# One-core Mamba block with a mixture of experts: five tables of slots respread (norms, outputs, experts' projections, scaled inputs)

## What is computed

```python
h = _layernorm(x) * (1 + ca) + sa
xn = layernorm(h) * norm_g + norm_b
# for each direction (forward, and backward on the flipped rows), 256 inner columns, 16 states:
u, z = split(xn @ Win.T);  u = silu(conv4(u) + convb)
dtr, Bm, Cm = split(u @ Wx.T);  dt = softplus(dtr @ Wdt.T + bdt)
h_t = exp(dt_t * A) * h_(t-1) + dt_t * u_t * B_t        # 512 steps
y_t = sum_n h_t * C_t;  y = (y + u * D) * silu(z) @ Wout.T
x = x + ga * (h + y_fwd + y_bwd)
h = _layernorm(x) * (1 + cb) + sb
w = top-2 softmax gates of h @ gate_w over 8 experts, 0 elsewhere
x = x + gb * (sum_e w_e * swiglu(h, ew1, ew2, ew3)[e] + swiglu(h, sw1, sw2, sw3))
```

## Time and profile before

| | us |
|---|---|
| median of 3 runs | 2438.02 (2435.1 to 2441.28) |
| the profiled execution | 2438.78 |
| its span | 2437.0 |
| PE, DVE, ACT, POOL busy | 2079.6, 2220.6, 1522.8, 2023.3 |
| granted TensorE clock, mean | 0.919 |

### The profile page before, as it was taken

The page is one execution under the profiler, slowest core; times in us unless marked ns, Lnnn a source line. Parts: engine busy times, 40 slices in busy tenths (PEclk is TensorE's granted clock), DMA queues, the critical chain, the costliest instruction groups (busy, mean ns, idle before and its releaser), DMA issues. The chain is left out here.

```text
span 2437.0 us, 32077 instructions
## 1 busy us (share of the span) xinstructions
PE 2079.6 (85%) x10085; PEld 1332.5 (55%) x10085; DVE 2220.6 (91%) x3530; ACT 1522.8 (62%) x2499; POOL 2023.3 (83%) x1334
## 2 busy tenths in 40 slices
PE   6678988889898888989888898888989888898868
PEld 2445655655565555655555565555656555565555
DVE  4999999999999999999999999999999999999952
ACT  4557666576666666666676666667665666666533
POOL 2768889888898898889889898988989899887845
PEclk7689989999898999989999998999989999998989
DMA  5333444433344433434343344343344333443410
GB/s 149 133 138 124 136 135 135 143 118 134 129 134 136 136 125 129 141 128 142 128 136 123 130 143 136 125 139 128 128 129 142 136 122 129 135 136 124 139 49 27
DMA packets 124061, 312.43 MB, mean 128 GB/s; under 512 B 19700, under 2 KB 46308, under 8 KB 123892
## 3 DMA queue, kind: packets, MB, share of 16 engines
q1 hardware_dynamic: 123892, 310.39, 38.1%
HBM read 303.74 MB, written 6.60 MB: 127 GB/s over the span
## 5 line engine op out<-in xcount | busy, mean ns | idle before, releaser
L495 POOL TENSOR_TENSOR bt<-v,bb 128x1024 f32<-128x1024 f32 x511 | 1205.2, 2360 | 104.3 <-DVE psA L941 89.7
L941 DVE TENSOR_TENSOR_SCAN psA<-psA,bt 128x512 f32<-128x512 f32 x1024 | 1195.8, 1213 | 83.1 <-ACT psA L680 65.3
L680 ACT ACTIVATE psA<-dt,aneg 128x512 f32<-128x512 f32 x1024 | 688.0, 688 | 591.8 <-DVE g L951 589.6
L1199 PEld LDWEIGHTS psY<-ident,g 128*128 128x128 f32 x4096 | 506.9, 150 | 495.2 <-DVE g L951 301.2
L1199 PE MATMUL psY<-ident,g 128*128 128x128 f32 x4096 | 602.2, 291 | 190.3 <-DVE g L951 189.2
L951 DVE TENSOR_TENSOR g<-psA,cb 128x512 f32<-128x512 f32 x1024 | 671.6, 675 | 0.0
L585 POOL TENSOR_TENSOR act<-pf,gf 128x512 f32<-128x512 f32 x288 | 366.1, 1271 | 171.7 <-DVE pf L1044 143.6
L1311 PE MATMUL F<-h2T,w 128*128 128x512 f32 x576 | 334.5, 664 | 91.7 <-DVE pf L1044 91.5
L1361 PE MATMUL F<-w,act 128*128 128x128 f32 x2304 | 308.5, 277 | 10.6 <-POOL act L585 10.5
L1361 PEld LDWEIGHTS F<-w,act 128*128 128x128 f32 x2304 | 281.9, 192 | 24.0 <-POOL act L585 18.2
L1215 PE MATMUL psP<-xnT,wcT 128*128 128x512 f32 x496 | 257.7, 645 | 0.1
(11 more groups left out here) (186 smaller groups left out, 1978.4 us busy)
## 6 DMA issues: line engine op xcount, KB each, us to landing
bb<-bc_rows SPq DMA_DIRECT2D x256, 512.0 KB, 3.7
cb<-bc_rows SPq DMA_DIRECT2D x256, 512.0 KB, 3.6
wB<-w_rows SPq DMA_DIRECT2D x80, 256.0 KB, 4.1
x<-in_L_attn_x SPq DMA_DIRECT2D x16, 256.0 KB, 4.4
out_x<-osb SPq DMA_DIRECT2D x16, 256.0 KB, 4.6
modA<-mod_table SPq DMA_DIRECT2D x15, 192.0 KB, 4.7
w<-in_L_ffn_ew SPq DMA_DIRECT2D x2, 1024.0 KB, 7.3
bc_rows<-xd SPq DMA_DIRECT2D x32, 64.0 KB, 3.3
```

The source lines that it names most:

```text
L495: g.tensor_tensor(bt[:, n % 2, :, :], v[d][:, :, :], bb[:, n // 2 % 2, n % 2, :].unsqueeze(1).broadcast_to([P, NH, T]), ALU.mult).then_inc ...
L680: s.activation(psA[:, half * T:half * T + T], dt_[d][:, half, :], ACT.Exp, scale=aneg[d][:, half, n:n + 1]).then_inc(a_s, 1)
L941: w.tensor_tensor_scan(ah, ah, bt[:, n % 2, half, :][:, order], 0.0, ALU.mult, ALU.add)\
L1199: last = m.matmul(psY[:, half * T + i * P:half * T + i * P + P], g_[:, n % 2, half, i * P:i * P + P], ident[:, :], is_transpose=True, star ...
```

## The change

Slots of pieces are changed, and with them the places of a few operations; no instruction is added or removed.

- Up projections: 7, 8, 10 to 21, 23 to 26 (before 7, 8, 11 to 21, 23 to 27). Downs: 10, 11, 13 to 22, 24 to 29 (before 10, 11, 14 to 22, 24 to 30); the weighted sums on DVE go with them to 14, 16, 18, the last sum to 29.
- TURN_SLOT 12 and ROWS_SLOT 13 (before 13, 14); scaled inputs in 15, 17, 19, 22, 23 (before 16, 18, 20, 22, 24).
- z of direction 0: both halves projected and turned in 30 (before 29, 30), both products in 31 (before 30, 31).
- Norms: 2, 3, 3, 4, 5, 6, 11, 13 (before 3, 4, 6, 7, 8, 9, 10, 12).
- POOL: both products of hx in 31 (before 23, 31), wg in 7 (before 6), output in 1 (before 0).
- SP: modF, modC and store move from slot 0 to slot 2, behind that slot's cb; x and modA stay in slot 0, now directly behind cb.
- PE's wait for wtsT stands in slot 13, before the transposes that reuse psP; TURN's own wait is now the last piece of direction 1.

```diff
--- before.py
+++ after.py
@@ -30,23 +30,24 @@
 PREP_SLOT = (19, 0)
 U_AT, XD_AT, DT_AT, LN1P_AT = 0, 6, 7, 9
 V_SLOT = (30, 12)
-Z_SLOTS, ZS_SLOTS = ((29, 30), (2, 5)), ((30, 31), (6, 6))
-STAT_SLOT, RSTD_SLOT, Z1_SLOT, H1_SLOT, STAT2_SLOT, RSTD2_SLOT, XNORM_SLOT, XN_SLOT = 3, 4, 6, 7, 8, 9, 10, 12
-HX_SLOTS, WG_SLOT = (23, 31), 6
+Z_SLOTS, ZS_SLOTS = ((30, 30), (2, 5)), ((31, 31), (6, 6))
+STAT_SLOT, RSTD_SLOT, Z1_SLOT, H1_SLOT, STAT2_SLOT, RSTD2_SLOT, XNORM_SLOT, XN_SLOT = 2, 3, 3, 4, 5, 6, 11, 13
+HX_SLOT, WG_SLOT = 31, 7
+OUT_SLOT, MODF_SLOT = 1, 2
 HALVE_SLOT = 13
 POST_F_SLOT = 17
 POSTB_SLOT, PROJ_SLOT, X2_SLOT, LN3_SLOT, H2T_SLOT, GATE_SLOT = 1, 3, 4, 4, 6, 7
 
 
-UP_SLOTS = [slot for slot in range(7, 28) if slot not in (9, 10, 22)]
-DOWN_SLOTS = [slot for slot in range(10, 31) if slot not in (12, 13, 23)]
+UP_SLOTS = [slot for slot in range(7, 27) if slot not in (9, 22)]
+DOWN_SLOTS = [slot for slot in range(10, 30) if slot not in (12, 23)]
 
 
 SCALED = 4
 NS = NE - SCALED
 SUMS = NT * (SCALED - 1) + 1
-TURN_SLOT, ROWS_SLOT = 13, 14
-XS_SLOTS = {16: 4, 18: 5, 20: 6, 22: 7, 24: 8}
+TURN_SLOT, ROWS_SLOT = 12, 13
+XS_SLOTS = {15: 4, 17: 5, 19: 6, 22: 7, 23: 8}
 
 
 def piece(d, kind, half=0):
@@ -415,14 +416,17 @@
                         elif scan and not last:
                             rows_in(b + 1, 0, (step - STEPS) // 2)
                     if slot == 0:
-                        early(b, scan, ffn, last)
+                        if scan and not last:
+                            load(b + 1)
+                    if ffn and slot == MODF_SLOT:
+                        ffn_rows(b - 1)
                     if ffn:
                         scales(b - 1, slot)
                     if scan and slot == X2_SLOT:
                         wait(sp, wg_s, b)
                         row = mod_dram[bass.ds(b, 1), 2 * D:3 * D].broadcast_to([P, D])
                         sp.dma_start(modG[:, :], row).then_inc(modG_in, 16)
-                    if slot == 0 and not (isinstance(b, int) and b < 2):
+                    if slot == MODF_SLOT and b >= 2:
                         store(b - 2)
 
             def scale_row(fb, e):
@@ -446,17 +450,13 @@
                 if e is not None and e + 2 < NE:
                     scale_row(fb, e + 2)
 
-            def early(b, scan, ffn, last):
-                if ffn:
-                    fb = b - 1
-                    wait(sp, o_s, 2 * fb)
-                    row = mod_dram[bass.ds(fb, 1), 5 * D:6 * D].broadcast_to([P, D])
-                    sp.dma_start(modF[:, :], row).then_inc(modF_in, 16)
-                    with nc.allow_non_contiguous_dma(reason="two columns"):
-                        sp.dma_start(modC[:, :], mod_dram[bass.ds(fb, 1), 3 * D:5 * D]
-                                     .rearrange("a (k p) -> p (a k)", p=P)).then_inc(modF_in, 16)
-                if scan and not last:
-                    load(b + 1)
+            def ffn_rows(fb):
+                wait(sp, o_s, 2 * fb)
+                row = mod_dram[bass.ds(fb, 1), 5 * D:6 * D].broadcast_to([P, D])
+                sp.dma_start(modF[:, :], row).then_inc(modF_in, 16)
+                with nc.allow_non_contiguous_dma(reason="two columns"):
+                    sp.dma_start(modC[:, :], mod_dram[bass.ds(fb, 1), 3 * D:5 * D]
+                                 .rearrange("a (k p) -> p (a k)", p=P)).then_inc(modF_in, 16)
 
             def store(fb):
                 sp.wait_ge(o_s, 2 * fb + 2)
@@ -521,11 +521,10 @@
                     g.tensor_tensor(xn[:, :, :], z1[:, :, :], over_tiles(modA[:, 1, :]), ALU.mult).then_inc(h1_s, 1)
                     pool.wait_ge(h1_s, 2 * b + 1)
                     g.tensor_tensor(z1[:, :, :], xn[:, :, :], over_tiles(modA[:, 0, :]), ALU.add).then_inc(h1_s, 1)
-                if slot == HX_SLOTS[0]:
+                if slot == HX_SLOT:
 
                     wait(pool, hxK_s, b)
                     g.tensor_tensor(hx[:, :, :], z1[:, :, :], over_tiles(modA[:, 2, :]), ALU.mult).then_inc(hx_s, 1)
-                if slot == HX_SLOTS[1]:
                     pool.wait_ge(hx_s, 2 * b + 1)
                     g.tensor_tensor(hx[:, :, :], hx[:, :, :], x[:, :, :], ALU.add).then_inc(hx_s, 1)
                 if slot == RSTD2_SLOT:
@@ -619,8 +618,7 @@
             norms(0, RSTD2_SLOT)
             pool.wait_ge(h1_s, 2)
             pool.wait_ge(ga_in, 16)
-            norms(0, HX_SLOTS[0])
-            norms(0, HX_SLOTS[1])
+            norms(0, HX_SLOT)
             pool.wait_ge(bt_s, 1)
             pool.wait_ge(bb_in[0], 16)
 
@@ -634,7 +632,7 @@
                         elif not last:
                             bmul.unit = 2 * b + 3
                             bmul(STEPS * b + nxt, 0, 0)
-                    if slot == 0 and not (isinstance(b, int) and b < 2):
+                    if slot == OUT_SLOT and b >= 2:
                         output(b - 2)
                     if scan:
                         side(b, slot, True, None if last else b + 1, True)
@@ -700,10 +698,10 @@
 
             def turn_z(b, d, slot):
 
-                if slot in Z_SLOTS[d]:
-                    half = Z_SLOTS[d].index(slot)
-                    act_e.wait_ge(z_full, 4 * b + 2 * d + half + 1)
-                    s.activation(th[:, 2 + half, :], (F0, F1)[half][:, :], ACT.Tanh).then_inc(zt_s, 1)
+                for half in range(NH):
+                    if slot == Z_SLOTS[d][half]:
+                        act_e.wait_ge(z_full, 4 * b + 2 * d + half + 1)
+                        s.activation(th[:, 2 + half, :], (F0, F1)[half][:, :], ACT.Tanh).then_inc(zt_s, 1)
 
             def prep(b, d, k):
 
@@ -1229,14 +1227,14 @@
 
             def project_z(b, d, slot):
 
-                if slot in Z_SLOTS[d]:
-                    half = Z_SLOTS[d].index(slot)
-                    if d == 0:
-                        wait(pe, (pf_s, F1_free)[half], 2 * NE * (b - 1))
-                    else:
-                        pe.wait_ge(z_free, 4 * b + half + 1)
-                    m.matmul((F0, F1)[half][:, :], wzT[d][:, half, :], xnT[:, PAD:PAD + T], start=True, stop=True)\
-                        .then_inc(z_full, 1)
+                for half in range(NH):
+                    if slot == Z_SLOTS[d][half]:
+                        if d == 0:
+                            wait(pe, (pf_s, F1_free)[half], 2 * NE * (b - 1))
+                        else:
+                            pe.wait_ge(z_free, 4 * b + half + 1)
+                        m.matmul((F0, F1)[half][:, :], wzT[d][:, half, :], xnT[:, PAD:PAD + T], start=True, stop=True)\
+                            .then_inc(z_full, 1)
 
             def skip_and_turn(bank, d, half):
 
@@ -1278,14 +1276,11 @@
                 if slot == TURN_SLOT:
 
                     pe.wait_ge(wts_s, 3 * fb + 3)
-                    if fb < NB - 2:
-                        pe.wait_ge(pP_free, xn_piece(fb + 2) + 1)
-                    else:
-                        pe.wait_ge(pP_free, min(PIECES * (fb + 1) + piece(1, DT, 1) + 1, PIECES * NB))
+                    pe.wait_ge(pP_free, min(PIECES * (fb + 1) + piece(1, DT, 1) + 1, PIECES * NB))
                     for i in range(NT):
                         last = m.transpose(psP[0:NX, i * P:i * P + P], wts[:, i, :], ident[:, :])
                     last.then_inc(turned, 1)
-                if slot == POST_F_SLOT:
+                if slot == XN_SLOT:
                     pe.wait_ge(wtsT_s, fb + 1)
 
             def expert_up(fb, slot):
```

## The result

The changed kernel takes 2528.93 us (median of 4 runs, 2525.2 to 2533.12) against 2436.56 for the kernel before in the same comparison: a ratio of 1.0377, 95% interval 1.0349 to 1.0405. It was forecast slower, at 2497 us, and the range ended at 2522: the sign was right and most of the waits stand where they were forecast, but the added time was 33 us short (92 us measured, 59 forecast), and the range did not hold the time. The profiled execution took 2525.22 us with a span of 2523.4, so 86.4 us of span were added.

The account below looks back on a forecast made before the run. VectorE was taken to bound the kernel, its waits setting the change: -0.9 + 0.3 + 2.7 + 0.35 + 0.8 + 0.6 + 0.1 = 3.95 us a body, times 15 = +59 us, giving 2497 us, range 2455 to 2522.

Parts of the forecast that it names:

- What bounds the kernel: VectorE, busy 91% of the span; its instructions stay, so time changes by its waits, 6.9 us in one body.
- Part 1, slots 28 to 30: Moving an up and a z half off slots 28 and 29 cuts waits around the Logarithm: 0.9 us a body saved.
- the drain that the Trainium skill states: ScalarE's switch of table set costs about 2.66 us with a drain; the prediction went by the trace instead.
- Part 2, slots 9 to 14: Moved normalization, statistics and turns: 0.2 off slot 11, later tanh at 9 and 12, slot 14; together +0.3 us a body.
- Part 3, the rows of weights: wB loads behind cb land late; the scaled input holds back slot 17's bt on GpSimd: +2.7 us a body.
- The rival by which SP's queue is not in the way: wB loads go out in slot 14 once w_rows has landed, taking 2.7 off: 2457 us; chance 0.08.
- The fixed part of 2.0 us: A DMA's fixed time by the Trainium skill; alone it would make the wB term about 0.6 us; not used.
- Part 4: Other scaled inputs moved on GpSimd: +0.35 us at scan 21, and 0.90 before scan 24 as it was.
- Part 5, x: x's statistics, a slot earlier in slot 2, wait for its load, median landing 4.4 us: +0.8, between 0 and 2.6.
- Part 5, x2: Statistics delay slot 2's gating and PE's projection, so x2 comes 1.55 us later: +0.6 us a body, between 0 and 1.6.
- "At nothing", bt of slot 1: GpSimd's dt, three bt, v and two hx in a row bring slot 1's bt to the edge: +0.1 us.

Follow-up runs that it names:

- the third experiment: The changed kernel with SP's loads of wB (slot 14) and of x and modA (slot 0) issued ahead of bb and cb: 2467.93 us, ratio 1.013.
- The first experiment: The changed kernel with the two wB loads of SP's slot 14 issued ahead of bb and cb: 2503.56 us, ratio 1.0279.
- the tenth: The changed kernel with SP's wB, x and modA loads ahead of bb and cb, and slot 16's copies of y behind the experts' turns: 2449.21 us, ratio 1.0053.
- the eleventh experiment: The changed kernel with SP's wB, x, modA loads first, x's statistics behind the gating, y's copies behind slot 16's turns, and slot edits: 2404.75 us, ratio 0.9873.
- the fifth experiment: The changed kernel with ups, downs, turn, rows and scaled inputs back in their earlier slots, xn's transposes in 14: 2499.97 us, ratio 1.0261.
- the sixth: The kernel before with only the change's ups, downs, turn, rows and scaled inputs, xn's transposes in 13 with PE's wait: 2477.66 us, ratio 1.0162.
- the ninth: The kernel before with only the change's experts' slots, and SP's slot 14 wB loads ahead of bb and cb: 2442.13 us, ratio 1.0017.

## Why the prediction was right in kind and short in size

- **What bounds the kernel:** right. VectorE's work stayed, and the time went where its waits went; the third experiment came out at its forecast time, 2468, from a sum of measured waits.
- **Part 1, slots 28 to 30:** right. 0.9 us a body was forecast; 0.23 + 0.86 + 0.23 = 1.32 against 2.38 is 1.06. No run has this part alone. The trace has the chain of table loads and Ln at 3.67 us again (1223.82 to 1227.49), so the drain that the Trainium skill states (ScalarE: Activation LUTs, What ACT_TABLE_LOAD costs) does not show in this kernel either.
- **Part 2, slots 9 to 14:** small and short. Forecast +0.3; measured +0.21 at 9, +0.22 at 12, +0.25 at 14 and nothing off slot 11, whose 1.69 stays: 0.7 in this body, 0.6 in the mean of fifteen. Taking the normalization and slot 8's statistics away from that Logarithm did not shorten its wait.
- **Part 3, the rows of weights:** right. The scaled input waited 3.9 to 4.3 us a body, and slots 16 and 17 together 3.24, less the 0.37 that stood before in 16 and 18: +2.9 against +2.7. Of this 0.37, the 0.22 us in slot 18 stood only in the one body from which it was read; in the other fourteen the gating of that slot waited 0.52 us for PE instead, and that wait is gone too. In the mean of the bodies it is 3.32 less 0.15 and 0.5, which is 2.7, so the exact agreement is in part luck. The first experiment took away the part of bt and left that of the tanh, as forecast; the tenth took that. The rival by which SP's queue is not in the way fell. The fixed part of 2.0 us that the prediction took from the Trainium skill (DMA: Bandwidth & Descriptors, Anatomy of one DMA) stands there for DMAs issued by GpSimd, and these go out from SP; the least landing of such a load stays 3.0 us here.
- **Part 4:** right, 0.32 at slot 21 and 0.91 at 24.
- **Part 5, x:** mis-sized. The median landing was taken, which gives 0.8 us. Most bodies waited 0.7 to 1.2, but four waited 1.6 to 2.8: the mean over the loads is 17.2 / 15 = 1.15. No wait was near zero. The landings are spread unevenly, in the changed kernel 4.3 us at the least, 4.5 the median and 6.4 at the most, so the mean wait lies above that of the median landing. (The upper bound given, 2.6, should be 2.7 by the landing of 6.3 that it rests on.)
- **Part 5, x2: the step that failed.** The prediction says that x2 "is copied 1.55 us later" and that its wait "becomes about 0.95", +0.6 a body and 9 us in all. Measured are 15.7 us of x2's waits and 3.5 of waits for the decays ahead of slot 4, behind the emptied slot 3, which the term was to hold: 19 us. Three things were wrong. First, what a gap does to PE was left out: the durations of its projections came from rows at the full clock, while the change first leaves PE idle there for 2.1 to 4.7 us. In three bodies the clock fell and x2 waited 2.35 to 3.84, 6 us more than three ordinary waits. Second, the terms named give 0.33 + 1.55 - 0.8 = 1.08 and not 0.95; the ordinary bodies have 0.88 + 0.23 = 1.11. Third, the 0.33 of before stood in about every second body only, 0.24 in the mean. In the profiled runs of other versions x2's waits sum to up to 37.6 us.
- **The term that was missing:** the sum adds waits by their length and puts what each does to the overlap of VectorE's instructions at nothing. Some 95 more waits of about 0.08 us are the 7.9 us of busy time that came in.
- **"At nothing", bt of slot 1:** a wait of 0.53 us for bt where 0.24 for the decays stood before, 0.3 where 0.1 was given. In the trace seven of GpSimd's pieces stand in a row from dt on (1226.31 to 1240.7), and dt waits 1.30 us for Ln, 0.17 before. In the eleventh experiment, with the first product of hx in slot 28, no wait for bt is left there.
- **The sum.** The profiled execution went up by 86.4 us against 59, 27 more. Above their forecast are x2 (10 us), the lost overlap (8), x (5), part 2 (5) and slot 1 (3), together 31. Against them, part 1 gave 1 more than forecast and some 3 us of waits behind the last scan are gone; parts 3 and 4 are at their forecasts. The gating's wait in slot 18 is there as before in the fifth experiment and not in the sixth and the ninth, so its going hangs on the experts' half. The median of the runs lies another 3.7 above the profiled one, whose group (2525) is one of two (2525 and 2533).
- **The range.** Each part had its bounds, and the upper ones of x, x2 and part 3 alone add 4.5 us a body. The range used 1.7 of them, as if the parts erred independently. Four terms came out above their middle (part 2, x, x2, slot 1) and none clearly below, and the lost overlap grows with each wait: the errors had one side in common.

## What to carry to other kernels

Where one engine's order is written by hand, ask of each piece that is moved up not only whether its own input is ready, but what stands behind it in its queue when it has to wait: the first scaled input cost nothing by its own lateness, and 2.2 us a body by the one bt behind it (2.1 in the body shown), which the first experiment gave back. A load in a queue of DMAs is as late as the wait of the load ahead of it, so what must come early has to be written ahead of the one that waits; two such swaps without another edit gave back 61 of the 92 us. Put into the sum the mean of a wait whose cause is spread unevenly, not the wait of the median, add what each new wait costs beyond its length, and if nearly all terms are waits, let the range reach further up than down.

## What the runs showed of the hardware that was not expected

TensorE's granted clock fell from 2.4 to 1.2 GHz after a gap of 1.8 to 5.1 us in some bodies and not in others with the same gap (1.76 us in the third experiment), so one wait took two values, 0.88 and 2.5 us, with none to 11 long ones in 15 bodies of a run. That may be why runs of the changed kernel lie in two groups 8 us apart (mean granted clock 0.925 and 0.926 in the faster two, 0.922 and 0.924 in the others); the runs other than the profiled one have no trace to show it. A scan or product that had to wait loses the 0.08 us by which it otherwise overlaps the one before: 7.9 us in all.
